# Weights and tokens laid out in DRAM as partitions take them, and row statistics of a recurrence from partial ones without transposes

## The reference, cut to what matters

```
k = rope(x @ Wk.T); v = x @ Wv.T          # 16 heads of 32
for each block of 16 tokens (32 blocks, one after the other):
    z = k_c @ W                            # W: 32x32 for each of 4 sequences x 16 heads
    W = W - k_c.T @ ((z - v_c) * inv_n)
out = layernorm(all z of a token, 512 features) * gamma + beta   # over all 16 heads
x1  = layernorm(x + out @ Wo.T)
x2  = layernorm(x1 + top-2 of 8 experts(x1) + shared_expert(x1))
```

## Time and profile before

| | |
|---|---|
| median of 3 runs | 717.73 us (717.64 to 718.1) |
| the profiled execution's own time | 717.65 us |
| its span, first to last instruction | 715.8 us |
| PE busy | 695.0 us, 97% |
| DVE, ACT, POOL busy | 64%, 48%, 46% |
| granted TensorE clock, mean | 0.994 of full speed |
| chain that ended last | PE 79%, DVE 10%, ACT 6%, issue 3% |
| DMA, mean | 144 GB/s, 59584 packets |

### The profile page before, as it was taken

The page is one execution under the profiler, slowest core; times in us unless marked ns, Lnnn a source line. Parts: engine busy times, 40 slices in busy tenths (PEclk is TensorE's granted clock), DMA queues, the critical chain, the costliest instruction groups (busy, mean ns, idle before and its releaser), DMA issues.

```text
span 715.8 us, 17650 instructions
## 1 busy us (share of the span) xinstructions
PE 695.0 (97%) x7388; PEld 583.7 (82%) x7388; DVE 461.5 (64%) x767; ACT 341.5 (48%) x662; POOL 330.0 (46%) x350
## 2 busy tenths in 40 slices
PE   9999999999999999999999999999999899999994
PEld 7767888788877777887888999999988878888883
DVE  4996564585755555378876676666576637767555
ACT  5654444454555442341123677767777542141232
POOL 3667556677555433011003665566574326526232
PEclk9999999999999999999999999999999999999998
DMA  8121131121242414000063798999788966414212
GB/s 291 66 75 47 47 104 47 62 89 34 105 135 76 150 47 147 29 14 1 0 235 103 239 326 291 311 319 327 253 274 259 317 189 196 119 68 118 74 73 89
DMA packets 59584, 102.86 MB, mean 144 GB/s; under 512 B 5296, under 2 KB 20400, under 8 KB 59504
## 3 DMA queue, kind: packets, MB, share of 16 engines
q1 hardware_dynamic: 53824, 83.11, 34.2%
q0 software_dynamic: 5680, 18.62, 8.5%
HBM read 79.95 MB, written 21.76 MB: 142 GB/s over the span
## 4 chain that ended last, share of the span: by engine, by line
PE 79%; DVE 10%; ACT 6%; issue 3%; POOL 0%; POOLq 0%; DVEq 0%; ACTq 0%
PE bank L755 20%; PE bank L444 12%; PE bank L779 10%; PE bank L1203 10%; PE bank L649 7%; PE bank L1250 5%; PE bank L573 4%; PE bank L548 4%; PE bank L1219 2%; PE bank L1176 2%; PE bank L684 2%; DVE GL L255 2%; ACT GH L254 2%; DVE sg L731 1%; ACT ah L254 1%
## 5 line engine op out<-in xcount | busy, mean ns | idle before, releaser
L231 POOL TENSOR_TENSOR xl<-RAW,xh 128x1024 fp32r<-128x1024 f32 x31 | 74.9, 2417 | 113.1 <-ACT xh L230 79.9
L254 ACT ACTIVATE ah<-sg 128x512 fp32r<-128x512 f32 (+1 forms) x64 | 33.6, 525 | 157.9 <-DVE sg L731 157.9
L755 PE MATMUL bank<-XH,GH 128*128 128x512 f32 x256 | 101.8, 398 | 1.5 <-ACT GH L254 0.9
L755 PE MATMUL bank<-XH,GL 128*128 128x512 f32 x256 | 99.9, 390 | 0.0
L755 PE MATMUL bank<-XL,GH 128*128 128x512 f32 x256 | 99.7, 389 | 0.0
L255 DVE TENSOR_TENSOR GL<-RAW,GH 128x1024 fp32r<-128x1024 f32 (+2 forms) x63 | 80.6, 1317 | 9.7 <-ACT GH L254 8.3
L591 POOL TENSOR_SCALAR rstd<-mv 128x1 f32<-128x1 f32 x48 | 15.3, 318 | 135.8 <-DVE mv L590 135.1
L1133 POOL DMA_INDIRECT xg<-x1d,idxu x39 | 49.9, 1281 | 57.0 <-DVE idxu L1114 41.2
L1203 PE MATMUL bank<-RH,GH 128*128 128x256 f32 x256 | 73.8, 288 | 0.8 <-ACT RAW L1260 0.4
L1203 PE MATMUL bank<-RH,GL 128*128 128x256 f32 x256 | 72.4, 283 | 0.0
L1203 PE MATMUL bank<-RL,GH 128*128 128x256 f32 x256 | 72.4, 283 | 0.0
(11 more groups left out here) (226 smaller groups left out, 1742.5 us busy)
## 6 DMA issues: line engine op xcount, KB each, us to landing
RAW<-in_wgu SPq DMA_DIRECT2D x21, 1024.0 KB, 8.6
RAW<-in_wd SPq DMA_DIRECT2D x21, 512.0 KB, 6.4
yd<-RAW SPq DMA_DIRECT2D x39, 256.0 KB, 7.5
RAW<-in_wsgu SPq DMA_DIRECT2D x14, 512.0 KB, 4.9
x<-in_xtok SPq DMA_DIRECT2D x16, 256.0 KB, 3.4
x1d<-x SPq DMA_DIRECT2D x16, 256.0 KB, 2.0
RAW<-in_wsd SPq DMA_DIRECT2D x8, 512.0 KB, 4.2
out_x<-x SPq DMA_DIRECT2D x16, 256.0 KB, 2.0
```

The lines of the kernel that those rows point to most:

```text
L231: b = PO.op(lambda e: e.tensor_tensor(DL[:, p, :, :], draw[:, rawp(w), :, :], DH[:, p, :, :].bitcast(F32), ALU.subtract), a, dloaded[w], *f)
L254: a = AC.op(lambda e: e.activation(hi, src, ACT.Copy), *tokens, *free)
L755: t = PE.op(lambda e, b=b, k=k, c=c, wt=wt, xx=xx, n=n: e.matmul(bank[b][:], wt[:, p, k, c:c + 128], xx[h][:, k, :], start=(n == 1), stop= ...
```

## The change

Two independent parts.

1. **Layout in DRAM.** The host lays out `xT`, `wgu`, `wd`, `wsgu` and `wsd` so that what one partition takes is one contiguous row (8 KB for gate-up weights and x, 4 KB for down weights). A load was made of rows of 2 KB (1 KB for the shared gate-up weights, which took two DMAs); now it is one DMA of 128 rows. `xT` of the first load keeps its 2 KB pieces.

2. **Row statistics.** `t_one` is gone, and with it the four PE transposes of a tile. In its place, in slot 4i+4 right behind `zt`, `stat_z` takes on DVE the statistics of the four groups of 128 values that lie in a partition (four `bn_stats`), writes them to DRAM (SP, 12 KB), and reads them back in four DMAs so that the four parts of a token come to lie in one partition. In slot 4i+6 `stats_one` no longer has its `bn_stats` over 512 values, but joins the four parts by one `bn_aggr`.

```diff
+        stz = part(pa, "late", "stz", [4, 6])
+        sta = part(pa, "late", "sta", [4, 6])
+        d_stz, d_sta = Stream(sem("d_stz")), Stream(sem("d_sta"))
+        zsd = nc.dram_tensor("zsd", (128, 4, 6), F32, kind="Internal").ap()
...
-            SP.dma(dst[:, :, 0:256], chunked(wsgu[:, n * 256:n * 256 + 256]), s)
-            gloaded[w] = SP.dma(dst[:, :, 256:512], chunked(wsgu[:, 1024 + n * 256:1280 + n * 256]), s)
+            gloaded[w] = SP.dma(dst, wsgu[n, :, :], s)
...
-            dloaded[w] = SP.dma(draw[:, p, :, :], chunked(wsd[n * 256:n * 256 + 256, :]), d_rawd[p])
+            dloaded[w] = SP.dma(RAW[:, p, 2048:3072], wsd[n, :, :], d_rawd[p])
...
-                    return e.dma_start(graw[:, p, :, :], wgu[bass.ds(which[w], 1), :, :].rearrange("a (k p) n -> p (a k) n", p=128))
+                    return e.dma_start(RAW[:, p, 0:2048], wgu[bass.ds(which[w], 1), :, :].rearrange("a p c -> p (a c)"))
...
-                    a, state.get("zT"))
+                    a, state.get("zread"))
...
-            state["zT"] = DV.op(lambda e: e.transpose(zT[:], ...), state["zst"], state.get("T1"), state.get("oh"))
-
-        def t_one(i):
-            b = 6
-            for g in range(4):
-                t = PE.op(lambda e, g=g: e.transpose(bank[b][:, g * 128:g * 128 + 128], zT[:, g * 128:g * 128 + 128], ident[:]),
-                          state["zT"], *free[b], inc=(g == 3))
-            state["T1"] = t
+            state["zT"] = DV.op(lambda e: e.transpose(zT[:], ...), state["zst"], state.get("oh"))
+
+        def stat_z(i):
+            for m in range(4):
+                t = DV.op(lambda e, m=m: e.bn_stats(stz[:, m, :], zst[:, :, m // 2, m % 2, :]), state["zst"], state.get("stz"))
+            state["zread"] = t
+            w = SP.dma(zsd, stz[:], d_stz, t, state.get("sta"))
+            state["stz"] = w
+            view = zsd.rearrange("(g r) m s -> m r g s", g=4)
+            for m in range(4):
+                state["sta"] = SP.dma(sta[32 * m:32 * m + 32, :, :], view[m], d_sta, w, state.get("n1a"))
...
-            state["n1"] = norm_stats(bank[6][:], state["T1"], 0)
-            free[6] = ((DV.sem, DV.count),)
+            b = DV.op(lambda e: e.bn_aggr(mv[:, 0, :], sta[:]), state["sta"])
+            state["n1a"] = b
+            c = PO.op(lambda e: e.tensor_scalar(rstd[:, 0, 0:1], mv[:, 0, 1:2], EPS, None, ALU.add), b)
+            state["n1"] = PO.op(lambda e: e.tensor_tensor(rstd[:, 0, 1:2], rstd[:, 0, 0:1], mhalf[:], ALU.pow), c, t_mh)
...
-        STAGES = [(3, False, fetch_x), (3, False, out_rows), (4, False, zt), (5, True, t_one), (5, False, hi_z), (6, False, residual),
+        STAGES = [(3, False, fetch_x), (3, False, out_rows), (4, False, zt), (4, False, stat_z), (5, False, hi_z), (6, False, residual),
```

More of the change, by code:

```diff
@@ L202, in fetch_down @@
                 def fetch_down(e):
-                    return e.dma_start(draw[:, p, :, :], wd[bass.ds(e.value_load(eid[0:1, n:n + 1], min_val=0, max_val=7), 1), :, :].rearrange("a (k p) n -> p (a k) n", p=128))
+                    return e.dma_start(RAW[:, p, 2048:3072], wd[bass.ds(e.value_load(eid[0:1, n:n + 1], min_val=0, max_val=7), 1), :, :].rearrange("a p c -> p (a c)"))
                 if n < FULL:
-                    SP.items.append(("i", lambda e: e.dma_start(draw[:, p, :, :], wd[bass.ds(which[w], 1), :, :].rearrange("a (k p) n -> p (a k) n", p=128)),
+                    SP.items.append(("i", lambda e: e.dma_start(RAW[:, p, 2048:3072], wd[bass.ds(which[w], 1), :, :].rearrange("a p c -> p (a c)")),
                                      sd.sem, 16))
@@ L283, in program @@
         wgs = part(pa, "late", "wgs", [4, 8])
-        part(pa, "late", "padl", [288])
+        stz = part(pa, "late", "stz", [4, 6])
+        sta = part(pa, "late", "sta", [4, 6])
+        part(pa, "late", "padl", [240])
         vst0 = sb(pa, "vst0", [8, 256])
@@ L612, in zt @@
         def zt(i):
-            state["zT"] = DV.op(lambda e: e.transpose(zT[:], zst[:].rearrange("p a b c d -> p (a b c d)")), state["zst"], state.get("T1"), state.get("oh"))
-        def t_one(i):
-            b = 6
-            for g in range(4):
-                t = PE.op(lambda e, g=g: e.transpose(bank[b][:, g * 128:g * 128 + 128], zT[:, g * 128:g * 128 + 128], ident[:]),
-                          state["zT"], *free[b], inc=(g == 3))
-            state["T1"] = t
+            state["zT"] = DV.op(lambda e: e.transpose(zT[:], zst[:].rearrange("p a b c d -> p (a b c d)")), state["zst"], state.get("oh"))
+        def stat_z(i):
[7 more added lines that the diff above has]
+                state["sta"] = SP.dma(sta[32 * m:32 * m + 32, :, :], view[m], d_sta, w, state.get("n1a"))
         def hi_z(i):
@@ L831, in slot @@
                 if loc == 3 and q + 2 < NB:
-                    xraw[q + 2] = SP.dma(xr[:], chunked(xT[:, (q + 2) * 512:(q + 2) * 512 + 512]), d_x, *(t for k in range(4) for t in xs[q + 1, k]))
+                    xraw[q + 2] = SP.dma(xr[:], xT[q + 2, :, :].rearrange("p (k n) -> p k n", k=4), d_x, *(t for k in range(4) for t in xs[q + 1, k]))
             if n == 43:
@@ L878, in slot @@
                 load_d(0)
-                load_g(1, graw[:, 0, :, :], d_raw[0])
+                load_g(1, RAW[:, 0, 0:2048], d_raw[0])
             if n == 50:
@@ L936, in program @@
         last_unit, halves = [None], [0]
-        xraw = {1: SP.dma(xr[:], chunked(xT[:, 512:1024]), d_x, *(t for k in range(4) for t in xs[0, k]))}
+        xraw = {1: SP.dma(xr[:], xT[1, :, :].rearrange("p (k n) -> p k n", k=4), d_x, *(t for k in range(4) for t in xs[0, k]))}
         last_unit[0] = tu[7]
@@ L1433 @@
     arrays = [
-        ("xT", xo.T), ("xtok", xo),
+        ("xT", xo.T.reshape(4, 128, 4, 512).transpose(2, 1, 0, 3).reshape(4, 128, 2048)), ("xtok", xo),
         ("wkT", np.asarray(inputs["L0_attn_Wk"]).T), ("wvT", np.asarray(inputs["L0_attn_Wv"]).T),
@@ L1438 @@
         ("bet", np.asarray(inputs["L0_attn_ln_beta"]).reshape(4, 128).T),
-        ("wg", inputs["L0_ffn_w_gate"]), ("wgu", inputs["L0_ffn_w_gate_up"]), ("wd", inputs["L0_ffn_w_down"]),
-        ("wsgu", inputs["L0_ffn_w_sh_gate_up"]), ("wsd", inputs["L0_ffn_w_sh_down"]),
+        ("wg", inputs["L0_ffn_w_gate"]),
+        ("wgu", np.asarray(inputs["L0_ffn_w_gate_up"]).reshape(8, 4, 128, 512).transpose(0, 2, 1, 3).reshape(8, 128, 2048)),
+        ("wd", np.asarray(inputs["L0_ffn_w_down"]).reshape(8, 2, 128, 512).transpose(0, 2, 1, 3).reshape(8, 128, 1024)),
+        ("wsgu", np.asarray(inputs["L0_ffn_w_sh_gate_up"]).reshape(4, 128, 2, 4, 256).transpose(3, 1, 0, 2, 4).reshape(4, 128, 2048)),
+        ("wsd", np.asarray(inputs["L0_ffn_w_sh_down"]).reshape(4, 2, 128, 512).transpose(0, 2, 1, 3).reshape(4, 128, 1024)),
         ("cos", c["cos"]), ("sin", c["sin"]), ("mask", c["mask"]), ("negi", c["negi"]),
```

6 lines of the change are left out of this document (3 added, 3 removed).

## The result

The changed kernel takes 723.88 us in the median of 4 runs (720.97 to 724.79), against 717.91 us for the kernel before in the same session: ratio 1.0085, 95% interval 1.0063 to 1.0107. In a second session it was 721.74 us against 716.41 us: 1.0077 (1.0056 to 1.0098). The prediction said slower, by 2.2 us; measured are 6.0 and 5.3 us, and 723.88 us lies 0.6 us above the end of its range.

What follows compares the result with a forecast made beforehand. PE, busy 695.0 of 715.8 us, was taken to bound the kernel. Its terms, -2.87 + 1.26 + 0.67 + 3 x 0.92 + 0.4 = +2.2 us on 717.65, gave 719.9 us, range 713.0 to 723.3 us.

Steps and rivals of the forecast that it cites:

- the sum itself: Whole kernel: the tile terms add up to +2.2 us on the profiled execution's 717.65 us, giving 719.9 us.
- tile 0: First tile: bn_aggr waits for the trip through DRAM, 0.39 us late, delaying a split PE waits for: +0.4 us.
- The transposes: PE, first stage: removing a tile's four transposes of z brings 0.41 us; seven tiles keep it, -2.87 us.
- the margins of tiles 3, 7, 10: Slack before PE starts: 0.29 us in tiles 3 and 7 (+1.26 us together), 0.25 us in tile 10 (+0.67 us).
- d: DVE, between `zt` and `stats_two` of the tile before: lateness from the four added bn_stats, 0.92 us.
- The trip's length: Statistics through DRAM: one store landing, four load issues and another landing take 5.7 us.
- Tile 15: End of the first stage: PE already waits for DVE's L782, so DVE's lateness passes through whole, +0.92 us.
- In the other tiles DVE has over a microsecond: Tiles after tile 0: DVE has room before needing the trip's result; only work needed a slot later stands behind.
- Layout: Weight loads: PE never waits for one, so the new DRAM layout gains 0, bounded by 0 and 1.0 us.
- stages behind 305 us: After the first stage: as long as before; a second stage over 1 us shorter would show the prediction wrong.
- Full-length bn_stats: DVE: the four start 0.31 us apart, 1.24 us in all, and lateness reaches PE: +5.0, 722.7 us; chance 0.16.
- a slow trip: Trip through DRAM: 24-byte rows make it 7.5 us, delaying PE in tile 0 and later splits: 722.6 us; chance 0.12.

Runs made afterwards that it cites:

- experiment 2: Three kernels against the changed one: the four bn_stats behind stats_two, 721.10 us; the same with bn_aggr a slot later, 716.14 us; bn_aggr a slot later alone, 718.33 us.
- the statistics alone: The kernel before with only the new row statistics, its DRAM layout and loads unchanged: 720.85 us, ratio 1.0058 to the kernel before.

## Why the prediction was wrong

**The step that failed is the sum itself: it had no term for the clock.** Its working ends at "717.65 + 2.2 = 719.9 us", as if a wait cost its own length. At full clock the change costs 2.3 us by its second session and 2.7 by the first (714.7 against 712.0), which is near the 2.2 of the sum. (For the first session the kernel before is taken from the later ones, where it was 711.8 to 712.1 us.) What was missing is 2.8 to 3.7 us of lower clock. It stands behind waits of some 2 us and more that the change makes: shown at the wait near 284 us, likely at tile 0. The second session's 721.74 us lies inside the range that was given, but what the sum lacks is missing there too: 5.3 us were measured against 2.2. The evidence lay in the profile before: a mean of 0.994, and the window shown above with one such fall behind a wait of the group in the earlier trace rows.

That the sum agrees so well at the full clock is in part luck, as the table shows: tile 0 cost 0.8 to 1.3 us above its term, and tiles 8 and 11, set at 0, brought 0.7 us.

**By tile** (the step of x1's transposes' start against before from one tile to the next, us; the profiles of the first and second session; the places are named as in the prediction, so that at "tile 2" stand the transposes of x1 of tile 1):

| tile | predicted | after | after, again |
|---|---|---|---|
| 0 and 1 | +0.4 - 0.41 | +1.82 | +0.75 |
| 2, 4, 5, 6, 9, 13 | -0.41 each | -0.35 to -0.40 | -0.36 to -0.41 |
| 3, 7 | +0.63 each | +0.54, +0.55 | +0.55, +0.53 |
| 8, 11 | 0 | -0.33, -0.40 | -0.33, -0.40 |
| 10 | +0.67 | +0.54 | +0.57 |
| 12 | +0.92 | +1.12 | +1.14 |
| 14 | +0.92 | +0.77 | +0.77 |
| 15, and up to the last | +0.92 | +2.37 | +2.36 |
| all | +2.2 | +4.69 | +3.63 |

- *The transposes* (0.41 us a tile) and *the margins of tiles 3, 7, 10* were right in place and size, by the rows.
- *d* was 0.92 us, measured 0.74 us: 0.19 us from start to start, nearer to the 0.15 of the earlier trace rows than to the line through both pairs. Each `bn_stats` is 0.27 us long and overlaps with the next. The Trainium skill ("VectorE: DVE Perf Modes", "Side-by-side" and the glossary's DRAIN) gave an estimate of 1.19 us, 0.30 for each. The length agrees nearly, with 0.27 us measured; that the next one waits for the pipe to be empty does not hold for these independent instructions, which start 0.19 us apart. Doing them twice moved PE's wait for the normalization by 0.80 us in tiles 3 and 7, which shows that d passes through in full once the margin is gone.
- *Tile 0* is the mis-sized term: +0.4 predicted, +2.2 and +1.2 measured, of which 0.5 in the first is the start of that execution. The trip's length was right (5.7 us; 5.66 and 6.16 measured), its parts less so: the stores of the earlier trace rows, called small in the prediction, are of 256 KB; the 12 KB here land after 1.4 us instead of 2.1, and the slowest of the loads after 2.8 and 3.3. What I left out is that DVE's splits behind it now meet POOL's 128x512 work and take 2.35 us instead of 1.29. The Trainium skill names such a collision ("GPSIMD Engine Reference", "1. Specifications": the two share their way to SBUF, and collide when a DVE instruction has two inputs there). This trace agrees: the split that starts beside POOL's L478 takes 1.76 us, the one ahead of it 0.68. In the kernel before it was POOL that was held up: L592, over one value in each partition, took 1.06 us beside the two splits, against 0.57 elsewhere, and L475 came only as they ended. That the meeting makes the difference is read from these rows; no run parts the two engines.
- *Tile 15* is +0.8 for DVE's lateness (+0.77 with `bn_aggr` later in experiment 2, where no fall followed) and 1.6 for the fall of the clock behind the 2.25 us.
- *"In the other tiles DVE has over a microsecond"* was wrong: `bn_aggr` waited 0.75 to 1.36 us in tiles 3, 7 and 10 as well. No wait of PE is seen behind it there, but moving the trip back by 1.5 us did at once (experiment 2).
- *Layout* at 0 was right. The *stages behind 305 us* took 1.4 and 1.0 us less than before (4.69 and 3.63 us in the table are 3.3 and 2.6 us at the end of the span), because they have no fall, and the kernel before had one there, 1.7 us. Read by their length alone they would have met a sign of being wrong that the prediction named, over 1 us shorter; at the full clock they are as long as before within 0.8 us.

**The rivals.** "Full-length bn_stats" gave 722.7 us and "a slow trip" 722.6, nearer to the time than the forecast, both for reasons that the traces refute (0.19 us apart; a trip of 5.7 to 6.2 us).

**Open.** Why the clock falls behind one wait and not behind another of the same length. In the fourteen profiles PE waits 26 times for 1.8 us or more; 16 of these waits have a fall behind them, and up to the tail of the program no fall stands anywhere else. Tile 0's 2.55 us had one in the profile of the statistics alone, its 2.49 us in that of the whole change had none, nor had 2.23 us at 279 us in experiment 2. And where the falls of a run without a profile lie is not known; their number is read from its mean clock.

## What to carry to other kernels

Where one engine bounds a kernel, a wait that a change puts on PE is priced at its length and, when it is about 2 us or more, at a possible fall of the clock on top (1.7 us each here, behind 16 of 26 such waits; the windows of the profile before already show one). Work taken off PE pays only in the tiles where PE waits for nothing else: count these before multiplying. And a trip through DRAM has a place for its start and one for its end: move either, and ask both who stands behind it and whether it is still in time.

## What the hardware showed that was not expected

- Added matmuls did not slow a kernel and probably made it faster: 9 of 0.23 us in the place of a wait, 721.74 to 719.88 us, with intervals that overlap a little. With eight in the place of a wait of 2.25 us the fall behind it was gone from the profile.
- Four independent `bn_stats` over 128 values start 0.19 us apart, each 0.27 us long (64 of them, 246 to 281 ns).
- A store of 128 rows of 96 bytes lands after 1.4 us and a load of 32 x 4 rows of 24 bytes after 1.8 us, four issues taking 1.75 us on SP: in the median tiny rows are no slower than the 2.0 us of the earlier trace rows, but single loads took up to 3.3 us.
- A DVE `tensor_tensor` over 128x512 that started beside a POOL one of the same size took 1.76 us, against 0.68 us; PE stood still for about 1 us more with it.
